# Adding sorted edges into adjacency tables: accumulation in groups of four tiles instead of two, with eight places per tile

## The reference

```python
ones = jnp.ones(src.shape[0], dtype=feat.dtype)
out_deg = jax.ops.segment_sum(ones, src, num_segments=N)
...
msg = feat[src] * ci[src, None]
agg = jax.ops.segment_sum(msg, dst, num_segments=N) * cj[:, None]
...
deg = jax.ops.segment_sum(w_a, dst_a, num_segments=n)
msg = h[src_a] * norm[:, None]
out = jax.ops.segment_sum(msg, dst_a, num_segments=n)
```

## Time and profile before

| | us |
|---|---|
| median of three runs | 2552.53 |
| lowest and highest | 2547.98, 2553.19 |
| the profiled execution | 2550.31 |
| its span | 2546.2 |
| table building inside the span | about 56 to 648 |
| VectorE busy in the whole span | 1458.0 (57%) |
| TensorE matmuls busy | 2003.1 (79%) |
| ScalarE busy | 1051.8 (41%) |

### The profile page before, as it was taken

The page is one execution under the profiler, slowest core; times in us unless marked ns, Lnnn a source line. Parts: engine busy times, 40 slices in busy tenths (PEclk is TensorE's granted clock), DMA queues, the critical chain, the costliest instruction groups (busy, mean ns, idle before and its releaser), DMA issues. The chain is left out here.

```text
span 2546.2 us, 47749 instructions
## 1 busy us (share of the span) xinstructions
PE 2003.1 (79%) x14338; PEld 1693.6 (67%) x14338; DVE 1458.0 (57%) x3333; ACT 1051.8 (41%) x2976; POOL 922.5 (36%) x884
## 2 busy tenths in 40 slices
PE   2888888888599999999988567777777777777772
PEld 1555555555379999999867356666667666666672
DVE  8999999999352111244232355555555555555555
ACT  5899999999331000011121333333333333333330
POOL 0022122212000000000000277777777777777771
PEclk9999999999699999999989555555555555555555
DMA  1467757766778887886745275555555555555541
GB/s 52 58 96 116 102 97 108 115 95 108 158 233 315 286 294 284 290 286 229 245 159 168 63 191 162 161 158 160 155 161 156 162 160 157 162 155 159 157 129 35
DMA packets 226412, 416.12 MB, mean 163 GB/s; under 512 B 131914, under 2 KB 151392, under 8 KB 216544
## 3 DMA queue, kind: packets, MB, share of 16 engines
q1 hardware_dynamic: 187485, 334.92, 48.8%
q0 software_dynamic: 38784, 79.48, 11.8%
HBM read 347.87 MB, written 66.43 MB: 163 GB/s over the span
## 5 line engine op out<-in xcount | busy, mean ns | idle before, releaser
L2230 POOL DMA_INDIRECT attention_windowed_vkv<-kv_dram,ttention_windowed_vsrc x808 | 778.1, 963 | 247.1 <-issue 218.0
L2313 PE MATMUL attention_windowed_vps_s<-attention_windowed_hot,attention_windowed_vmsg 128*104 128x32 f32 x1616 | 321.9, 364 | 273.3 <-DVE attention_windowed_vmsg L2370 272.5
L2313 PEld LDWEIGHTS attention_windowed_vps_s<-attention_windowed_hot,attention_windowed_vmsg 128*104 128x104 f32 x1616 | 295.6, 288 | 311.7 <-DVE attention_windowed_vmsg L2370 271.1
L651 ACT ACTIVATE add_edges_hot_lo<-add_edges_hot_lo,add_edges_parts 128x128 bf16<-128x128 bf16 x1616 | 487.3, 387 | 26.0 <-DVE add_edges_hot_lo L759 23.4
L689 PE MATMUL add_edges_ps_pair<-add_edges_hot,add_edges_hot_lo 128*128 128x300 bf16 x2424 | 441.9, 292 | 0.0
L2301 PE MATMUL attention_windowed_vps_e<-attention_windowed_vwe,attention_windowed_vattr 97*128 97x96 f32 x1616 | 404.3, 432 | 24.7 <-ACT attention_windowed_hot_T L2258 24.7
L1224 PE MATMUL graph_layers_acc<-graph_layers_w_tab,graph_layers_g 125*96 125x125 f32 x3750 | 417.7, 270 | 0.0
L1224 PEld LDWEIGHTS graph_layers_acc<-graph_layers_w_tab,graph_layers_g 125*96 125x96 f32 x3750 | 406.7, 163 | 0.0
L2301 PEld LDWEIGHTS attention_windowed_vps_e<-attention_windowed_vwe,attention_windowed_vattr 97*128 97x128 f32 x1616 | 368.9, 334 | 25.7 <-issue 25.7
L683 PE MATMUL add_edges_ps_pair<-add_edges_hot,add_edges_hot_lo 128*128 128x300 bf16 x808 | 238.3, 295 | 108.3 <-DVE add_edges_strip L790 62.7
L2263 ACT ACTIVATE attention_windowed_vmsg<-ttention_windowed_vscore 128x32 f32<-128x32 f32 x202 | 46.3, 229 | 656.8 <-DVE ttention_windowed_vscore L2366 653.6
(11 more groups left out here) (233 smaller groups left out, 2158.0 us busy)
## 6 DMA issues: line engine op xcount, KB each, us to landing
graph_layers_w_tab<-w_blocks SPq DMA_DIRECT2D x75, 1562.5 KB
graph_layers_c_tab<-c_blocks SPq DMA_DIRECT2D x75, 800.0 KB, 4.4
w_blocks<-add_edges_strip SPq DMA_DIRECT2D x25, 1562.5 KB, 17.6
attention_windowed_vattr<-in_attr_T SPq DMA_DIRECT2D x202, 192.0 KB, 2.7
attention_windowed_vdrow<-dstf_dram SPq DMA_DIRECT2D x202, 192.0 KB, 3.1
c_blocks<-add_edges_counts SPq DMA_DIRECT2D x25, 800.0 KB, 16.2
attention_windowed_vkv<-kv_dram,ttention_windowed_vsrc POOLq DMA_INDIRECT x808
ttention_windowed_q_rows<-q_dram SPq DMA_DIRECT2D x202, 18.0 KB, 2.6
```

The source lines that it names most:

```text
L651: done = nc.scalar.activation(hot_lo[s][:, 1 + part, j, :], hot_lo[s][:, 0, j, :], ACT.Copy, scale=parts[:, part, bass.ds(g * G + j, 1)])
L2230: nc.gpsimd.indirect_dma_start(out=kv[s][:, k, :], out_offset=None, in_=kv_dram, in_offset=bass.IndirectOffsetOnAxis(ap=src4[s][:, k:k + 1 ...
L2313: last = nc.tensor.matmul(ps_s[s % 2][:], msg[s][:, k, :], hot[s][:, k, :], start=k == 0, stop=k == Q4 - 1)
```

## The change

WINDOW becomes 8, so `hot` has 200 columns instead of 300, and a place is the destination less the first destination of its own tile. Four tiles share one PSUM buffer `ps_four` with REACH = 20 nodes for each of the 25 source tiles (500 columns, one bank for each table). Every matmul writes its 25 x 8 columns at a start inside the 20 that TensorE reads from a register: `in_reach`, the distance from the first node of the four to the first node of the tile, cut off at 12. What is cut off is added to the place. Because the eight columns of a tile don't cover the bank, two matmuls of zeros over 500 columns open each group of four, and all others accumulate. VectorE adds 2 x 25 x 20 elements per four tiles, twice per batch, and `strip` gets 20 columns behind its ring. The second weight part of the last four tiles of a batch is made on VectorE (`middle`) and no longer on ScalarE (BY_ACT = 4). `examine_edges` computes `in_reach` and the places; `ps_base` and its matmul go.

```diff
-WINDOW = 12
+WINDOW = 8
+REACH = 20
...
-        strip = mem.sb("strip", [P, 2, NT, RING + WINDOW])
+        strip = mem.sb("strip", [P, 2, NT, RING + REACH])
...
-                        for part in range(2):
+                        for part in range(2 if j < BY_ACT else 1):
...
-                    for j in range(4):
-                        p = 4 * g + j
-                        if j % 2 == 0:
-                            pe.wait_ge(hot_ready, 2 * g + 1 + j // 2)
-                        pe.wait_ge(parts_ready, p + 1)
-                        if reaches(p, 2):
-                            pe.wait_ge(added, p - 1)
-                        out = ps_pair[j % 2]
-                        for m in range(2):
-                            e = 2 * j + m
-                            nc.tensor.matmul(out[:, 0, 0:PLACES], hot_lo[s][:, 0, e, :], hot[s][:, e, :], start=m == 0, stop=m == 1)
+                    at = spots(g)
+                    for u in range(2):
+                        q = 2 * g + u
+                        pe.wait_ge(hot_ready, q + 1)
+                        if reaches(q, 2):
+                            pe.wait_ge(added, q - 1)
+                        both = ps_four[u]
+                        for table in range(2):
+                            nc.tensor.matmul(both[:, table, 0:NT * REACH], nought[:], noughts[:], start=True, stop=False)
+                        for m in range(Q4):
+                            e = Q4 * u + m
+                            if m % 2 == 0:
+                                pe.wait_ge(parts_ready, 4 * g + e // 2 + 1)
+                            cells = both[:, :, 0:NT * REACH].rearrange("p c (t n) -> p c t n", n=REACH)[:, :, :, bass.ds(at[e], WINDOW)]
+                            nc.tensor.matmul(cells[:, 0], hot_lo[s][:, 0, e, :], hot[s][:, e, :], start=False, stop=m == Q4 - 1)
...
-                                last = nc.tensor.matmul(out[:, 1, 0:PLACES], hot_lo[s][:, 1 + part, e, :], hot[s][:, e, :],
-                                                        start=m == 0 and part == 0, stop=m == 1 and part == 2)
+                                last = nc.tensor.matmul(cells[:, 1], hot_lo[s][:, 1 + part, e, :], hot[s][:, e, :],
+                                                        start=False, stop=m == Q4 - 1 and part == 2)
...
+            nc.vector.tensor_copy(middle2[:], piece[:].unsqueeze(2).broadcast_to((P, ET, 2)))
...
+            def middle(g, s):
+                n, m = P // 2, G - BY_ACT
+                table = middle2[:, bass.ds(g * G + BY_ACT, m), :].unsqueeze(2).broadcast_to((P, m, n, 2))
+                nc.vector.tensor_tensor(pairs(hot_lo[s][:, 2, BY_ACT:G, :], n), pairs(hot_lo[s][:, 0, BY_ACT:G, :], n), table, ALU.mult)
...
-            def add(p, j, at):
-                cells = strip[:, :, :, bass.ds(at, WINDOW)]
+            def add(q, u, at):
+                cells = strip[:, :, :, bass.ds(at, REACH)]
...
-                    add(4 * g + 3, 3, at[3])
```

More of the change, by code:

```diff
@@ L531, in add_edges @@
         third2 = mem.sb("third2", [P, ET, 2], BF16)
+        middle2 = mem.sb("middle2", [P, ET, 2], BF16)
         hi = mem.sb("hi", [P, ET], BF16)
@@ L539, in add_edges @@
         tile_of = mem.sb("tile_of", [P, NT + 1], BF16)
-        ones = mem.sb("ones", [1, P])
+        nought = mem.sb("nought", [1, P], BF16)
+        noughts = mem.sb("noughts", [1, NT * REACH], BF16)
         zero = mem.sb("zero", [P, 1])
-        start = mem.sb("start", [1, NPAIR])
-        turn = mem.sb("turn", [1, NPAIR])
-        ring_col = mem.sb("ring_col", [1, NPAIR], I32)
-        ps_pair = [mem.ps(f"ps_pair{s}", [P, 2, BANK]) for s in range(2)]
+        start = mem.sb("start", [1, NQ])
+        turn = mem.sb("turn", [1, NQ])
+        ring_col = mem.sb("ring_col", [1, NQ], I32)
+        ps_four = [mem.ps(f"ps_four{s}", [P, 2, BANK]) for s in range(2)]
         ps_odeg = mem.ps("ps_odeg", [P, NT + 1])
-        ps_base = mem.ps("ps_base", [P, NPAIR])
         loaded = mem.sem("loaded")
@@ L666, in _, with spots @@
         def _(pe):
-            pe.wait_ge(ones_ready, 1)
-            nc.tensor.matmul(ps_base[:], ones[:], pair_first[0:1], start=True, stop=True).then_inc(base_ps, 1)
+            pe.wait_ge(noughts_ready, 2)
+            def spots(g):
+                why = "the first node of the place of a tile in the reach of its four, cut off at its end"
+                _, at = nc.values_load_multi_w_load_instructions(in_reach[0:1, bass.ds(G * g, G)], engines=(mybir.EngineType.PE,), min_val=0,
+                                                                 max_val=REACH - WINDOW, skip_runtime_bounds_check_because=why)
+                return at
             def body(r, rm, batches):
@@ L805, in body @@
                     dve.wait_ge(cleared, 2 * (r - 2))
-                ats = columns(4 * r - 2 + batches[0], 4 * len(batches))
+                ats = columns(4 * r - 2 + batches[0], 2 * len(batches))
                 for k in batches:
@@ L825, in body @@
                         third(g + 1, s)
+                        middle(g + 1, s)
                     if folds:
[L827 removed]
+                        dve.wait_ge(added, 2 * g + 1)
                         fold(r)
                         dve.wait_ge(folded, 2 * ((r - 2) // SLOTS_B) + 1)
[L830 to L835 removed]
+                        if more:
+                            places(g + 1, s, 0)
+                        nc.vector.memset(strip[:, :, :, RING:RING + REACH], 0.0).then_inc(folded, 1)
                         finish(r, rm)
+                        if more:
+                            places(g + 1, s, 1)
                         dve.wait_ge(folded, 2 * ((r - 2) // SLOTS_B) + 2)
                         dve.wait_ge(block_done, r - 1)
[L839 to L840 removed]
+                    elif more:
+                        places(g + 1, s, 0)
+                    add(2 * g + 1, 1, at[1])
+                    if more and not folds:
                         places(g + 1, s, 1)
[L842 removed]
             lanes(0, 0)
@@ L880, in graph_layers @@
         h = [mem.sb(f"h{s}", [P, D]) for s in range(2)]
+        y = [mem.sb(f"y{s}", [P, D]) for s in range(2)]
+        z = mem.sb("z", [P, D])
         aggT = [mem.sb(f"aggT{s}", [D + 1, LANES]) for s in range(2)]
@@ L898, in graph_layers @@
         pos = mem.sb("pos", [P, NT])
-        y = [mem.sb(f"y{s}", [P, D]) for s in range(2)]
-        z = mem.sb("z", [P, D])
         st = mem.sb("st", [P, 6])
```

69 lines of the change are left out of this document (31 added, 38 removed).

## The result

| | before | after |
|---|---|---|
| time, median | 2552.53 us | 2566.63 us (2556.91 to 2580.61, 15 runs) |
| ratio to before | | 1.0056, 95% interval 1.0039 to 1.0074 |
| profiled execution, span | 2546.2 us | 2567.4 us |
| table building, last block's step | 647.3 us | 666.3 us |

The account below looks back on a forecast made before the run. VectorE was taken to bound the table building. 65 us saved, less 17 for stalls, 12 for clock or store, 3 for longer folds and 4 for setup, left 29: median 2523 us, range 2502 to 2555.

Parts of the forecast that it names:

- What bounds the kernel: Table building, 592 of 2546 us: VectorE, busy 582.5, sets the pace; TensorE follows and ScalarE is close behind.
- VectorE's saving: Table building: a VectorE batch falls from 5.63 to 4.99 us, 0.64 saved times 101 batches, 65 us.
- rival 4: More gain: no stall and folds hidden give 2495 us, or 2505 with a third of stalls and waits left; 9%.
- The stall in each batch: VectorE waits for TensorE's four tiles: 2.44 us against 2.10, taken as 0.25 each; minus 17 us, from 7 to 41.
- my 69: Stalls counted in table building: 18 plain rounds with 3, six fold rounds with 2, and 3 at the ends.
- The clock: Fold rounds: TensorE's clock falls or the store is late, about 2 us per fold round; minus 12 us, 0 to 25.
- rival 3: Clock falls between any two groups; at 1.2 GHz for the whole table building the time would pass 2742 us; 3%.
- The sequencer: TensorE's register loads and address computations per batch and tile: taken as covered, below 0.08 us per register-addressed matmul.
- rivals 1 and 2: Register-addressed matmuls or loads cost TensorE more: gain partly eaten, 2535 to 2548 us, 20%; or slower, 2646 at 0.15, 9%.
- The middle part on VectorE: 512 bf16 elements per batch move from ScalarE to VectorE, adding 0.33 us to VectorE's batch.
- falls off the path: ScalarE drops from 16 to 12 scalings a batch, 17.1 us a round against some 20.7; no gain counted.
- Fold rounds: Six rounds: the weights' store and clearing let the next round start after 24.2 us, VectorE ready after 23.2; longer folds minus 3.

Follow-up runs that it names:

- e9: Changed kernel with TensorE's loop over one round, zero matmuls ahead of the wait, 128-row zero operands, and VectorE's tiles ahead of the addition: 2487.5 us, 0.9761 of before.
- e7: Changed kernel with TensorE's loop written over one round and zero operands of 128 rows instead of one: 2515.3 us, 0.9864 of before.
- e6: Changed kernel with TensorE's loop written over one round (20 turns) instead of four: 2534.4 us, 0.9941 of before.
- e4: Changed kernel with each tile's columns at a place fixed in the code instead of in a register, register loads kept: 2527.7 us, 0.9920 of before.
- e5: Changed kernel unedited, run again on a second chip as anchor: 2552.0 us, 1.0012 of before.
- e12: Changed kernel with all second parts made by ScalarE again and no middle on VectorE: 2558.5 us, 1.0033 of before.
- e11: As e10, with the middle part of two tiles more back on ScalarE (six there, two on VectorE): 2481.5 us, 0.9732 of before.
- e10: As e9, with VectorE making the first half of the next places before the fold in fold rounds: 2485.7 us, 0.9750 of before.

## Why the prediction was wrong, step by step

**What bounds the kernel, and VectorE's saving: right.** The pitches of addition, half of the places and middle are 1.106, 0.485 and 0.335 against estimates of 1.107, 0.482 and 0.33; a batch is 4.997 against 4.99. The 65 us are there. When nothing eats them, in e9, the kernel is 63 us faster than before (61 by the ratio); my own rival 4 (no stall, folds hidden) had 58, without the change of order.

**The stall in each batch: right mechanism, too small a term.** I took 0.25 us where the sum of rows gave 0.34, because the tail had been read at half the clock. Measured at full clock are 0.48 in the median of 61 such places (most 0.33 to 0.65; the batch shown above has 0.40), and 0.38 with zeros of 128 rows (e7, 75 places). Two pieces were missing: the zeros take 0.52, not 0.42 (0.09 is the switch of rows), and the tail hardly shrank at full clock: from 304.12 three tiles end at 305.23, the addition comes at 305.59, 0.36 later against 0.41. As for the number, 79 losses stood between the lanes and the addition, against my 69. Tiles of 0.44 us, below, add what is left in some batches. The 0.09 shaved off a value that the rows gave was some 6 us over 69 batches. The term of 17 us measured some 33.

**The clock: right place, too small a term, and a place missing.** I charged it to the six folds, 12 us with all else there, and gave "between any two groups" 3%, with the argument that TensorE's busy share is nearly the same as before. The slow clock did begin behind folds, and behind the turns, which I hadn't seen; but it lasted up to 23.9 us, and what VectorE lost in it is some 28 us more than before. The busy share is indeed the same; but part of it is now two matmuls of one row. With 128 rows in the same columns the slow clock was 17 instead of 68 us (e7 against e6). The mean of 0.99 in rows 1 belonged to a kernel whose matmuls all had 128 rows and could not speak for the new ones. "PEclk below 0.9 over the stretch" was my sign for rival 3: it was 0.92 over the loop and 0.88 from 400 to 600, so the sign came only in a part of it. The rival itself didn't come true: nine of the ten spells begin behind a fold or a turn, and one elsewhere.

**The sequencer: looked at in the wrong unit, and the step without a term.** I asked what an address costs per tile and found it hidden up to 0.08 us a matmul. That was nearly right: at full clock three of four tiles follow at 0.37 to 0.38 and one at 0.44 to 0.45, which was my sign for rivals 1 and 2; with fixed addresses (e4) none takes 0.44. e4 against e6 has it at some 5 us, with overlapping intervals and on two chips. What I didn't count was the length of the code: 384 more instructions in a loop of 1,443, and four jumps back of 3.4 us each, worth 17.6 us (e6 against e5). No term and no rival had it. The register load of 0.59 to 1.9 us mostly lies in TensorE's pause, as I said, but stands behind the branch at each turn; no run takes it away.

**The middle part on VectorE: costed right, and needed.** Undone in e12 it gives 1.0033 instead of 1.0012. The 33 us that it costs on VectorE can't be had back this way, because ScalarE then has 21.7 us of work in each round and becomes the pace. That ScalarE "falls off the path" by it was right. e11 shows that a smaller part on VectorE is somewhat better.

**Fold rounds: the store is not what is last.** VectorE waited for the clearing twice in the loop, 1.7 us in all. The fold's pause on TensorE does matter, by the clock it lowers: five of the ten slow spells begin there. Making the places first (e10) changed nothing by then.

**The account, and the steps that failed.** Between the loops of the two profiled executions: VectorE's pitches 101 x 0.64 = minus 65; losses in front of its instructions 93 instead of 14, plus 79; longer folds plus 4; the first lanes 1.8 later. That is plus 20, and the loop ended 19.0 later. By where they lie in the trace, the 79 are about 33 in batches at full clock, 28 under slow clock and 15 at the loop's turns; the rest I can't place. The forecast had 17, 12 and nothing. So three steps failed, each by some 15 us, and none of them alone makes the miss of 44: the stall was taken at half its size, the clock's fall was priced as if the new matmuls were like the old, and the length of the loop's code had no term.

## What to carry to other kernels

An edit that adds instructions to a hardware loop can have a price that no duration of an instruction in its body shows: count the loop body's instructions on each engine and look at the branch's row and the code queue's packets before and after. A helper matmul that only sets PSUM to zero is better written with as many rows as its neighbours, as e7 and e9 have it, and ahead of the wait for the data, since behind it its columns lie on the path of the first consumer. And when a busy engine becomes shorter, the slack of the one that follows it shrinks by as much: price the chain from the producer's last instruction to the consumer's first with the value that the rows give, not with a kinder one. Before a run with a part undone is read as "this part is worth nothing", look whether the engine that took the part over is now busy without a pause.

## What the runs showed of the hardware

- A branch that jumps back on TensorE took some 0.21 us with 458, 1,443 and 1,550 recorded instructions in the body, and 3.3 to 3.9 us with 1,811 and 1,827; in the long ones a packet of 16 KB on q8 begins 0.9 to 1.0 us after the branch.
- Two zero matmuls of 500 columns with one row, before a matmul of 128 rows: 0.52 us from start to start; with 128 rows 0.43.
- The granted clock went from its upper level (2.4 GHz) to the lower one behind pauses of TensorE of 2.2 to 2.6 us in both e6 and e7; with one-row zeros it stayed there for 6.8 to 17.1 us, with 128-row zeros for 3.4 us or not at all, with the columns the same and the pauses no shorter.
- A matmul of 200 columns whose address comes from a register follows its neighbour mostly at 0.084 to 0.086 us, and in a part of the tiles at 0.09 to 0.11: tiles of 0.37 and of 0.44 us. With fixed addresses (e4) it is 0.085 and there are no tiles of 0.44. That the slow ones are those not queued during a wait would fit; no run shows it.
